# A graph network kernel of four layers: each gather of five edge passes waits for the one two ahead of it, in place of a wait for all at every sixth or eighth

## What is computed

```python
h_src = table[src]                             # one row of a table for each edge: the gather
e = leaky_relu(alpha_s[src] + alpha_d[dst])    # gat: scores, then a softmax over each node's edges
msg = where(edge_type == r, x_src @ W[r], 0)   # rgcn: the row depends on source and relation
out = segment_sum(msg * weight, dst)           # sums over the edges of one destination
```

## Time and profile before

| | |
|---|---|
| median of three runs | 27904.17 us |
| the profiled execution, own time | 27881.0 us |
| its span in the profile | 27879.0 us |
| busy: PE, DVE, POOL | 22584.5, 18896.7, 17266.8 us |
| gathers of both gat passes on POOL, L999 | 4464 of 948 ns in the mean |
| gathers of both rgcn passes, L739 | 3968 of 946 ns |
| gathers of typed_e, L2773 | 1984 of 954 ns |

### The profile page before, as it was taken

One profiled execution on the slowest core, in us unless ns is written; L12 is line 12 of the kernel. 1 busy time (PEld: TensorE's weight loads), 2 busy tenths in 40 slices (PEclk: granted clock), 3 DMA queues, 4 the chain that ended last, 5 costly groups with the idle time before them and its releaser, 6 DMA issues. The chain is left out here.

```text
span 27879.0 us, 524081 instructions
## 1 busy us (share of the span) xinstructions
PE 22584.5 (81%) x200772; PEld 19283.5 (69%) x200772; DVE 18896.7 (68%) x47358; ACT 1533.6 (6%) x3291; POOL 17266.8 (62%) x15844
## 2 busy tenths in 40 slices
PE   0788866888867999969999388888888887299996
PEld 0677763444436888858888388888888887088886
DVE  3788875555555777757777366666666666388886
ACT  0000000000000000000000011111111111100000
POOL 1555556666655555545656377777777778455555
PEclk9999987999977999979999699999999998599998
DMA  4222221111111111111111122222222222522221
GB/s 77 65 64 64 64 60 28 40 40 40 40 33 33 34 34 34 34 29 32 32 32 31 20 39 34 39 34 39 34 39 34 39 34 30 130 60 61 61 61 43
DMA packets 1659413, 1234.13 MB, mean 44 GB/s; under 512 B 1258171, under 2 KB 1501045, under 8 KB 1615189
## 3 DMA queue, kind: packets, MB, share of 16 engines
q0 software_dynamic: 870816, 181.33, 10.4%
q1 hardware_dynamic: 676340, 582.52, 7.6%
q10 hardware_dynamic: 110016, 437.07, 4.0%
HBM read 736.61 MB, written 462.67 MB: 43 GB/s over the span
## 5 line engine op out<-in xcount | busy, mean ns | idle before, releaser
L919 PE MATMUL gat_e_found<-gat_e_parts,gat_e_lowhot 128*128 128x224 bf16 (+1 forms) x41664 | 5873.2, 305 | 1108.7 <-DVE gat_e_rows L888 866.5
L2324 PE MATMUL sheaf_e_found<-sheaf_e_parts,sheaf_e_lowhot 128*128 128x238 bf16 x46872 | 5319.3, 274 | 1063.3 <-DVE sheaf_e_rows L2159 439.0
L919 PEld LDWEIGHTS gat_e_found<-gat_e_parts,gat_e_lowhot 128*128 128x128 bf16 x41664 | 4127.0, 101 | 2854.5 <-DVE gat_e_rows L888 909.8
L2085 POOL DMA_INDIRECT bysrc<-sheaf_e_toadd,sheaf_e_torow x3224 | 5175.9, 1605 | 1490.9 <-issue 839.5
L999 POOL DMA_INDIRECT gat_e_rows<-att_t,gat_e_index x4464 | 4233.2, 948 | 2716.5 <-DMA gat_e_rows<-att_t,gat_e_index 1462.6
L2324 PEld LDWEIGHTS sheaf_e_found<-sheaf_e_parts,sheaf_e_lowhot 128*128 128x128 bf16 x46872 | 4711.8, 102 | 1518.3 <-issue 651.7
L739 POOL DMA_INDIRECT rgcn_e_rows<-rel_t,rgcn_e_index x3968 | 3751.9, 946 | 2831.1 <-DMA rgcn_e_rows<-rel_t,rgcn_e_index 1518.3
L1815 PEld LDWEIGHTS rgcn_e_found<-rgcn_e_parts,rgcn_e_lowhot 128*128 128x128 bf16 x52080 | 5033.8, 99 | 573.6 <-issue 512.0
L1815 PE MATMUL rgcn_e_found<-rgcn_e_parts,rgcn_e_lowhot 128*128 128x224 bf16 x52080 | 5239.2, 263 | 105.4 <-issue 99.4
L2773 POOL DMA_INDIRECT typed_e_rows<-typed_t,typed_e_index x1984 | 1893.0, 954 | 1434.3 <-DMA typed_e_rows<-typed_t,typed_e_index 910.0
L919 PE MATMUL typed_e_found<-typed_e_parts,typed_e_lowhot 128*128 128x224 bf16 x26040 | 2658.9, 263 | 135.0 <-issue 77.1
(11 more groups left out here) (491 smaller groups left out, 21822.9 us busy)
## 6 DMA issues: line engine op xcount, KB each, us to landing
sheaf_e_allsrc<-src_d ACTq DMA_DIRECT2D x62, 1664.0 KB
sumsatt<-gat_e_sums ACTq DMA_DIRECT2D x62, 1404.0 KB
rgcn_e_low<-low_d SPq DMA_DIRECT2D x124, 640.0 KB
typed_e_types<-in_type_t SPq DMA_DIRECT2D x62, 1280.0 KB, 7.8
typed_t<-typed_p_y SPq DMA_DIRECT2D x98, 765.0 KB
gat_e_rows<-att_t,gat_e_index POOLq DMA_INDIRECT x4464
sheaf_e_low<-low_d SPq DMA_DIRECT2D x62, 1152.0 KB
sumsatt<-gat_e_sums ACTq DMA_DIRECT2D x62, 1092.0 KB
```

Source lines behind the costliest of these rows:

```text
L919: last = pe.matmul(self.found_ps[n % 2][:, c, 0:self.width * NHI], hot[:, k, col * P:(col + 1) * P], self.table.column(part, k), start=par ...
L2085: pool.indirect_dma_start(g.by_src[k][r], rows(to_row[k][:, j:j + 1]), to_add[k][:, j, 0:FD], None, compute_op=ALU.add).then_inc(summed[k] ...
L2324: last = pe.matmul(found_ps[n % 2][:, c, 0:W * NHI], hot[:, k, col * P:(col + 1) * P], short.column(part, k), start=part == 0 and k == 0, ...
```

## The change

The semaphore of each buffer set becomes two, one for gathers of even columns and one for those of odd columns (the class `Landings` with `in_flight` 2). Ahead of each gather but the first two of a chunk, POOL waits until the gather two columns before has landed (`hold`), and adds one to `g.gate`. The waits at every sixth or eighth column are gone. Whoever waited for a whole chunk (SP, DVE) now waits for both semaphores (`all_of`). Nothing else changes: the same gathers, in the same order, into the same buffers. The edits of `typed_attention_pass` and `relation_pass` are those of `attention_pass` shown here.

```diff
+IN_FLIGHT = 2
-DRAIN = 6
-LONG_DRAIN = 8
...
-def drain_some(pool, g, gathered, turn, cols, j, each=DRAIN):
-
-    if j > 0 and j % each == 0:
-        pool.wait_ge(gathered, turn * (16 * cols) + 16 * j)
-        pool.sem_inc(g.gate, 1)
+class Landings:
+
+
+    def __init__(self, s, cols, in_flight):
+        self.slots, self.cols = in_flight, cols
+        self.landed = [[s.sem(f"landed{k}{r}") for r in range(in_flight)] for k in range(2)]
+        self.per = [len(range(r, cols, in_flight)) for r in range(in_flight)]
+
+    def sem(self, k, j):
+        return self.landed[k][j % self.slots]
+
+    def all_of(self, eng, turn, k):
+
+        for sem, n in zip(self.landed[k], self.per):
+            eng.wait_ge(sem, turn * (16 * n) + 16 * n)
+
+    def hold(self, pool, g, turn, k, j):
+
+        if j >= self.slots:
+            r = j % self.slots
+            pool.wait_ge(self.landed[k][r], turn * (16 * self.per[r]) + 16 * (j // self.slots))
+            pool.sem_inc(g.gate, 1)
...
     def gather_column(self, pool, table, k, j):
         pool.indirect_dma_start(self.rows[k][:, j, :], None, table, rows(self.index[k][:, j:j + 1]))\
-            .then_inc(self.gathered[k], 16)
+            .then_inc(self.landings.sem(k, j), 16)
...
         for j in range(self.cols):
-            drain_some(pool, g, self.gathered[k], turn, self.cols, j)
+            self.landings.hold(pool, g, turn, k, j)
             self.gather_column(pool, table, k, j)
...
     def wait_rows(self, dve, i, k):
-        dve.wait_ge(self.gathered[k], i * (16 * self.cols) + 16 * self.cols)
+        self.landings.all_of(dve, i, k)
...
-        each = LONG_DRAIN if kinds else DRAIN
...
                     if not fresh:
-                        sp.wait_ge(gathered[k], i * (16 * JG))
+                        landings.all_of(sp, i - 1, k)
                     sp.dma_start(index[k][:, :], chunk(g.src_id, i, k)).then_inc(index_in[k], 16)
...
                     for j in range(JG):
-                        drain_some(pool, g, gathered[a.k], a.turn, JG, j, each)
+                        landings.hold(pool, g, a.turn, a.k, j)
                         pool.indirect_dma_start(rows_t[a.k][:, j, :], None, table, rows(index[a.k][:, j:j + 1]))\
-                            .then_inc(gathered[a.k], 16)
+                            .then_inc(landings.sem(a.k, j), 16)
...
-                    dve.wait_ge(gathered[k], i * (16 * JG) + 16 * JG)
+                    landings.all_of(dve, i, k)
                     f.all_taken(dve, a)
...
-        b = EdgeBuffers(s, g, FD, index_d, extras, FD, JP)
+        b = EdgeBuffers(s, g, FD, index_d, extras, FD, Landings(s, JP, IN_FLIGHT))
```

More of the change, by code:

```diff
@@ L693, in scan_max, with __init__ @@
     return dve.tensor_tensor_scan(out, penalty, values, before, ALU.add, ALU.max)
-def drain_some(pool, g, gathered, turn, cols, j, each=DRAIN):
-    if j > 0 and j % each == 0:
-        pool.wait_ge(gathered, turn * (16 * cols) + 16 * j)
-        pool.sem_inc(g.gate, 1)
+class Landings:
[13 more added lines that the diff above has]
+            pool.sem_inc(g.gate, 1)
 class EdgeBuffers:
-    def __init__(self, s, g, table_w, index_d, extras, sums_w, cols=J):
-        self.index_d, self.extras, self.cols = index_d, extras, cols
+    def __init__(self, s, g, table_w, index_d, extras, sums_w, landings):
+        self.index_d, self.extras, self.landings, self.cols = index_d, extras, landings, landings.cols
         self.rows = [s.sb(f"rows{k}", [P, J, table_w]) for k in range(2)]
@@ L712, in __init__ @@
         self.sums = [s.sb(f"sums{k}", [P, J, sums_w]) for k in range(2)]
-        self.index_in, self.extra_in, self.gathered, self.used, self.done, self.stored = (
+        self.index_in, self.extra_in, self.used, self.done, self.stored = (
             [s.sem(f"{n}{k}", c) for k in range(2)] for n, c in
-            (("index_in", 0), ("extra_in", 0), ("gathered", 0), ("used", 0), ("done", 1), ("stored", 16)))
+            (("index_in", 0), ("extra_in", 0), ("used", 0), ("done", 1), ("stored", 16)))
         self.stage = s
@@ L724, in turn @@
                 if not first:
-                    sp.wait_ge(self.gathered[k], i * (16 * self.cols))
+                    self.landings.all_of(sp, i - 1, k)
                 sp.dma_start(self.index[k][:, :], chunk(self.index_d, i, k)).then_inc(self.index_in[k], 16)
@@ L959, in attention_pass @@
         dve_o, rows_used, done, dropped, raised = (s.sem(n) for n in ("dve", "rows_used", "done", "dropped", "raised"))
-        index_in, edges_in, gathered, stored = ([s.sem(f"{n}{k}") for k in range(2)]
-                                                for n in ("index_in", "edges_in", "gathered", "stored"))
+        index_in, edges_in, stored = ([s.sem(f"{n}{k}") for k in range(2)]
+                                      for n in ("index_in", "edges_in", "stored"))
+        landings = Landings(s, JG, IN_FLIGHT)
         acc = by_edge(sums_d)
@@ L1632, in turn @@
                     if not fresh:
-                        sp.wait_ge(b.gathered[k], i * (16 * JP))
+                        b.landings.all_of(sp, i - 1, k)
                     sp.dma_start(b.index[k][:, :], chunk(b.index_d, i, k)).then_inc(b.index_in[k], 16)
@@ L2771, in gather @@
                     for j in range(JG):
-                        drain_some(pool, g, gathered[a.k], a.turn, JG, j)
+                        landings.hold(pool, g, a.turn, a.k, j)
                         pool.indirect_dma_start(rows_t[a.k][:, j, :], None, table, rows(index[a.k][:, j:j + 1]))\
-                            .then_inc(gathered[a.k], 16)
+                            .then_inc(landings.sem(a.k, j), 16)
                 for k in range(2):
```

## The result

The changed kernel takes **29542.5 us** (median of 4 runs, 29493.24 to 29561.26), the kernel before 27907.55 us in the runs beside it: a ratio of 1.0583, 95% interval 1.0568 to 1.0597. I had forecast 28800 us, and at most 29200. The sign was right; the loss forecast, 896 us, was little more than half of the 1635 that came. The profiled execution took 29556.69 us, with a span of 29555.0.

A forecast was written before the change was run, and what follows sets the result against it. POOL's gathers were taken to pace most passes. Pass losses of 155, 422, 0, 118 and 127 us plus 74 for code made 896 on a profiled 27881.0; with 23 for the median, 28800 us, range 28500 to 29200.

The forecast's parts named there:

- What bounds the passes: POOL's gathers pace gat1_e, gat2_e and rgcn1_e, and typed_e after some turns; in rgcn0_e POOL waits for DVE.
- The quiet sum: Gathers with quiet DMA queues: 3.15 us a pair, chunks 49.5 to 49.75 us, in gat2_e 57.6 to 62.35.
- the rival of a hidden wake-up: POOL's holds in all passes: a pair needs only 2.44 us, no hold binds, 26960 us; chance 0.05.
- The new hold: POOL's gathers: each waits for the one two before, 3.15 us from start to start of every second gather.
- Half of the burst is lost: Load and store bursts in the passes: a pair takes 6.3 us in place of 3.15, losing half the burst.
- POOL's pace would be about that of rgcn1_e, 52.3 us, below DVE's 53.8: rgcn0_e: DVE's slower pace covers POOL's longer chunk, so the change costs 0 us.
- The term of 74 us: Added hold code: two more instruction-fetch gaps of 1.2 us, 31 turns each, +74 us; bounds 0 and 150.
- 155, 422, 0, 118 and 127 us: Losses forecast for gat1_e, gat2_e, rgcn0_e, rgcn1_e and typed_e, in that order.
- longer bursts: Rival for bursts in the passes: they cost three quarters of their length, 1507 us more, 29410 us; chance 0.08.
- My own upper bounds by term: Upper limits: 7.2, 12 and 4.4 us a chunk in gat1_e, gat2_e, rgcn1_e; 420 us typed_e; 150 us added code.

The follow-up runs named there:

- e10: Changed kernel with each pair's landing hold replaced by a 128 x 8 POOL fill and the wait for it: 28023.89 us, 1.0035 of the kernel before.
- e2: Changed kernel with three gathers in flight instead of two: 38061.04 us, ratio 1.2705 to the kernel before.
- e3: Changed kernel with four gathers in flight instead of two: 39045.9 us, ratio 1.304 to the kernel before.
- e1: Changed kernel with both semaphores kept but the old waits at each sixth or eighth column: 30038.85 us, ratio 1.0033 to the kernel before.
- e4: Changed kernel with PE multiplying only the first of three table parts in both gat passes and typed_e: 29457.99 us in one profiled run.
- e15: Changed kernel with 128 x 8 POOL fills replacing holds, at each third gather in gat2_e, each second elsewhere: 27960.4 us, 0.9464 of the kernel before.
- e5: The kernel before, unchanged, profiled on another chip: 29565.1 us, median of its runs there.

## Why the prediction was wrong

Point by point:

- **What bounds the passes: right.** Both gat passes, rgcn1_e and typed_e lost what POOL lost.
- **The quiet sum (3.15 us a pair, 49.75 and 62.35 us a chunk): right.** The pair takes 3.14 to 3.19 in the median of the passes. e10 has nearly the same pair without landings, at 50.6 and 63.3 us a chunk with 0.8 and 1.0 us for the stall. The wake-up is real: 0.80 us behind each landing that was waited for, and 0.81 behind POOL's own fill, so the rival of a hidden wake-up is out. The landing comes 2.4 us after a gather's start, as I had worked out.
- **The step that failed is "The new hold. A gather can now start only when the one two before has landed", priced with the landing of a quiet gather everywhere but in bursts.** A gather has landed when the slowest of its 16 parts has. A wait at each sixth gather depends on little more than the last landing of the six; the holds look at all, and in four of five passes one in six to eight is late. Against POOL's pace without landings (50.5 us, 63.3 in gat2_e) the changed kernel pays 8.7, 4.1, 4.7, 4.7 and 9.4 us a chunk. Late parts outside bursts are 3.4, 0.1, 3.1, 3.9 and 2.5 of it, and I had nothing for them. With those in bursts they are at most 5.8, 0.2, 3.6, 4.1 and 4.9. So the bursts cost between 2.9 and 5.3 us in gat1_e, between 3.9 and 4.0 in gat2_e, 1.1 to 1.6 and 0.6 to 0.8 in the rgcn passes, and 4.5 to 6.9 in typed_e; my chunks held 5.9, 3.1, 2.6, 2.6 and 6.2. "Half of the burst is lost" was thus too little in gat2_e, too much in both rgcn passes, and about right or too much in the other two.
- **rgcn0_e, "POOL's pace would be about that of rgcn1_e, 52.3 us, below DVE's 53.8", put at 0: wrong** by the same step. Both passes do have the same pace, but it is 55.2, so DVE's cover was gone: 52 us.
- **The term of 74 us for what "looks like the fetch of the next block of instructions": mis-sized.** The stall costs some 240 us in five passes. It comes every 96 or 80 gathers, 20 or 30 times a pass, and takes 2.34 or 1.95 us where I took 1.2. The kernel before already paid part of that, 31 x 1.2 = 37 us in gat2_e by the earlier trace rows, so the change added some 200. That it is such a fetch no run shows.
- **By pass** I had 155, 422, 0, 118 and 127 us, with 74 beside them, 896 in all; measured 376, 549, 52, 295 and 373, 1645 in all. The rival "longer bursts", 29410 us, came nearest to the time, but for another reason. My own upper bounds by term add up to about 29.9 ms; the range stopped at 29200, as if the terms would not all err to the same side. They did, since one cause sits in four of them.
- **Missed, in the sum and in the rivals:** that the kernel before stands close to a cliff, with its 27904 us just above the edge on some chips and 29.6 ms part of the way down on others. Without pauses PE is slowed: e2 takes 27% more time, e3 30%.

What isn't shown: what a late part inside a burst costs, beyond the bounds above; why PE is slowed; and what sets the chips apart. The sets of e1 to e4 and of e15 ran on the same chip, and the kernel before took 29949 us in the one and 29553 in the other, so it is not the chip alone.

## What to carry to other kernels

A wait for a transfer costs what its slowest part costs, so the more often it is placed, the more of the rare late ones it meets; price it by the tail of the landings, and not by the quiet median. A wait that looks like pure loss may be pacing an engine for another's sake: before it is thinned out or moved, try the kernel with it doubled and with it halved. If pacing is what is wanted, pace by something short of one's own (here a fill of 0.13 us and the wait for it), which gave the same pause without the landings and won 5% where the kernel before was slowed. And measure before and after on more than one chip when a kernel stands near such a cliff.

## What was not expected of the hardware

- While POOL issues gathers 1.25 us apart without a pause, PE's instructions start one each 1.4, 2.1 or 2.8 us, multiples of 0.70, with nothing awaited (739.3 us of 2000 in e2, against 60.7 with a hold at each second). It begins after 7 to 13 gathers in half of the chunks of gat1_e, after 12 in gat2_e. A pause of 0.81 to 0.95 us at each second gather prevents all or nearly all of it; at each third or fourth it does not in passes of 32 columns.
- The same kernel takes 27.9 or 29.6 to 30.0 ms by the chip and the time. 1390 of 1667 us between e5 and the first profile are in the passes where PE is slowed, the rest elsewhere; the kernel with the short pauses took 28.0 and 28.5.
- In 12 to 18% of the gathers of four passes one of the 16 parts lands about 1 us behind the others, and with it the gather: 98% of these overlap an instruction fetch, 17% of the others do, and with 270 of the fetches gone they fell from 18 to 6.7%.
- A gather of POOL starts 0.80 us after the landing it waits for, and 0.81 us after the end of POOL's own fill that it waits for; a fill of 128 x 320 instead of 128 x 8 adds 444 us to DVE's busy time over some 4900 fills.
